# Last layer of a four-layer network: key times value formed in token rows, the scan banks filled by transposes that shift by one token

## The reference, cut to what matters

```python
def step(s, rkvw):
    r_t, k_t, v_t, w_t = rkvw
    a = k_t[:, :, :, None] * v_t[:, :, None, :]
    out = jnp.einsum('bhk,bhkd->bhd', r_t, u * a + s)
    return (a + w_t[:, :, :, None] * s, out)
```

## Time and profile before

| | us |
|---|---|
| runs shown: median (lowest to highest, 3 runs) | 1236.12 (1231.64 to 1236.43) |
| the profiled execution, its own time | 1234.46 |
| span of its profile | 1232.6 |
| PE busy in the span | 1107.8 (90%) |
| DVE busy | 837.0 (68%) |
| ACT busy | 541.0 (44%) |
| POOL busy | 426.9 (35%) |

### The profile page before, as it was taken

How to read it: one execution, slowest core, us unless ns; L and a number is a source line. 1 busy time by engine, 2 the same in 40 slices (tenths; PEclk the granted TensorE clock), 3 DMA queues, 4 the chain that set the end, 5 groups by cost and what they waited for, 6 DMA issues and landing times. The chain is left out here.

```text
span 1232.6 us, 21261 instructions
## 1 busy us (share of the span) xinstructions
PE 1107.8 (90%) x7840; PEld 703.0 (57%) x7840; DVE 837.0 (68%) x1609; ACT 541.0 (44%) x1000; POOL 426.9 (35%) x387
## 2 busy tenths in 40 slices
PE   7987788999999899999899899888998998989966
PEld 5875566568567567567567568564442433523414
DVE  4655766866866865866866866854467697695764
ACT  4643464473473473473473474441304314314221
POOL 2111444343343333343333333322335255164240
PEclk9979898999999999999999999999998999989988
DMA  7220100000001010102000000210010010000100
GB/s 243 64 91 18 40 1 23 18 18 19 20 17 56 17 60 17 34 17 87 19 17 21 17 17 18 71 62 18 1 35 19 1 36 18 18 19 1 34 1 17
DMA packets 37375, 40.73 MB, mean 33 GB/s; under 512 B 8064, under 2 KB 32832, under 8 KB 37072
## 3 DMA queue, kind: packets, MB, share of 16 engines
q1 hardware_dynamic: 37200, 40.01, 10.2%
q0 software_dynamic: 128, 0.10, 0.0%
HBM read 31.71 MB, written 8.39 MB: 33 GB/s over the span
## 5 line engine op out<-in xcount | busy, mean ns | idle before, releaser
L1349 DVE TENSOR_REDUCE b_neg_max<-head_area 128x16 f32<-128x1024 f32 x64 | 77.9, 1216 | 87.1 <-POOL head_area L784 86.7
L2054 POOL TENSOR_TENSOR c_rs<-c_st,head_area 128x512 f32<-128x512 f32 x64 | 82.2, 1286 | 129.9 <-DVE c_st L2462 129.9
L789 POOL TENSOR_TENSOR b_rstd<-b_var,minus_half 128x1 f32<-128x1 f32 x63 | 34.6, 549 | 256.6 <-DVE b_var L1378 256.6
L1032 PE MATMUL ps<-b_hT_mlp,wl 128*128 128x512 f32 x224 | 108.8, 608 | 8.4 <-ACT b_hT_mlp L1165 7.2
L1200 ACT ACTIVATE head_area<-head_area 128x1024 f32<-128x1024 f32 x64 | 68.0, 1062 | 102.2 <-DVE head_area L1354 101.6
L1046 PE MATMUL ps<-w,b_act_g 128*128 128x256 f32 x448 | 104.4, 387 | 2.7 <-ACT b_act_g L1218 2.7
L784 POOL TENSOR_TENSOR head_area<-head_area,b_self_add 128x1024 f32<-128x1024 f32 x32 | 75.7, 2366 | 81.7 <-DVE head_area L1342 81.7
L784 POOL TENSOR_TENSOR head_area<-head_area,b_cross_add 128x1024 f32<-128x1024 f32 x32 | 75.5, 2359 | 80.6 <-DVE head_area L1342 80.6
L1205 ACT ACTIVATE head_area<-ps 128x512 f32<-128x512 f32 x128 | 70.3, 605 | 63.9 <-PE ps L980 63.9
L1046 PEld LDWEIGHTS ps<-w,b_act_g 128*128 128x128 f32 x448 | 84.0, 193 | 18.1 <-issue 4.6
L865 PE MATMUL ps<-head_area,wl 128*128 128x512 f32 x176 | 86.2, 613 | 2.0 <-SPq L681 2.0
(11 more groups left out here) (252 smaller groups left out, 2319.8 us busy)
## 6 DMA issues: line engine op xcount, KB each, us to landing
b_x_in<-x_mid SPq DMA_DIRECT2D x9, 512.0 KB, 3.8
wl<-in_wl SPq DMA_DIRECT2D x4, 1024.0 KB, 6.8
head_area<-in_ctxT SPq DMA_DIRECT2D x8, 512.0 KB, 3.7
x_mid<-b_x_out SPq DMA_DIRECT2D x8, 512.0 KB, 2.9
area<-in_wc SPq DMA_DIRECT2D x1, 2336.0 KB, 8.3
a_x_in<-in_x SPq DMA_DIRECT2D x16, 128.0 KB, 3.1
a_y_in<-in_ctx SPq DMA_DIRECT2D x16, 128.0 KB, 3.5
w<-in_w SPq DMA_DIRECT2D x2, 1024.0 KB, 9.5
```

The source lines that it names most:

```text
L1032: mm = pe.matmul(ps[:, YB + j % 2, :], weight("w1", k, j * P, (j + 1) * P), hT_mlp[:, k, :], start=(k == 0), stop=(k == NC - 1))
L1349: dve.tensor_reduce(neg_max[:, k % 2, :], t, AX, ALU.max, negate=True).then_inc(max_ok, 1)
L2054: pool.tensor_tensor(rs[:, i % 4, :], st[:, i % 3, :], rF[:, i // RS, :], ALU.mult).then_inc(rs_ok, 1)
```

## The change

The product of k and v is formed with tokens on the rows, and the banks of the scan are filled by transposes of the product.

- ACT copies k and v without the extra column (`kF`, `vF`). PE transposes both to token rows (`to_tokens`, 4 transposes per chunk of channels, so 16 per head), and ACT copies these four outputs to `k_tok` and `v_tok` (`copy_tokens`). A head has 15 outputs, not 11. Both are placed in the turn and in the block between the phases.
- DVE forms the product of all 8 value channels for 128 tokens in one instruction of 128x1024 elements (both inputs repeated by their access patterns). The four instructions of the first chunk of channels stand in the turn before `own_weight`, those of the second chunk after the scans 0 to 3.
- `spread_v` with one selection product is replaced by `update` with four transposes. Their second operand is not the identity but `next_token`, which moves each token by one within its sequence. `key_value` on the PSUM bank is gone; the scan follows `start_state` directly.
- Two memsets (of `kS` and `vS`), the matrix `sel` (8 by 128 columns) and one semaphore of `phase_a` go. Some tiles of the middle layers move into shared areas; their waits stay as they were.

```diff
-HEAD = ("xx", "maa", "x5", "dec", "dexp", "decay", "kS", "vS", "rF", "gg", "ruk")
-OUTS = 11
+HEAD = ("xx", "maa", "x5", "dec", "dexp", "decay", "kF", "vF", "rF", "gg", "ruk", "k_tok", "v_tok", "kv1")
+OUTS = 15
+FIRST_OUT = {"k": 3, "k_tok": 5, "v": 7, "v_tok": 9, "r": 11, "g": 13}
...
 # phase_a: inv_ok joins xvn_ok
-                dve.reciprocal(inv, row_sum[:, p, :]).then_inc(inv_ok, 1)
-                dve.wait_ge(inv_ok, t + 1)
+                dve.reciprocal(inv, row_sum[:, p, :]).then_inc(xvn_ok, 1)
+                dve.wait_ge(xvn_ok, 2 * t + 1)
...
 # phase_c, bank_free (the block before phase_c alike)
-                    pe.wait_ge((k_ok, v_ok, r_ok)[(old - 3) // 2], NC * n + (old - 3) % 2 + 1)
+                    c = (old - 3) % 2 + 1
+                    if FIRST_OUT["k_tok"] <= old < FIRST_OUT["v"]:
+                        pe.wait_ge(tok_ok, 2 * NC * n + c)
+                    elif FIRST_OUT["v_tok"] <= old < FIRST_OUT["r"]:
+                        pe.wait_ge(tok_ok, 2 * NC * n + NC + c)
+                    else:
+                        pe.wait_ge({"k": k_ok, "v": v_ok, "r": r_ok}[...], NC * n + c)
...
-            def spread_v(n, i):
-                c = place(i)[0]
+            def to_tokens(n, src, done, m):
+                for c in range(NC):
+                    pe.wait_ge(done, NC * n + c + 1)
+                    bank_free(n, m + c)
+                    for p in range(NP):
+                        mm = pe.transpose(ps[:, PROJ + (m + c) % 2, p * P:(p + 1) * P], src[:, c, p * P:(p + 1) * P], w["ident"][:, :])
+                    mm.then_inc(proj_ps, 1)
+
+            def update(n, i):
+                c, d = i // RS, 2 * (i % 4) + i % RS // 4
                 if i >= 4:
                     pe.wait_ge(st_ok, NS * n + i - 3)
-                pe.matmul(seqs(ps[:, VB[i % 4], :]), w["sel"][:, i % RS, :], vS[:, c, :, 0:S], start=True, stop=True).then_inc(vb_ps, 1)
+                if i % RS == 0:
+                    pe.wait_ge(kv_ok, NC * NP * n + NP * (c + 1))
+                for p in range(NP):
+                    mm = pe.transpose(ps[:, VB[i % 4], p * P:(p + 1) * P], kv[c][:, p, d * P:(d + 1) * P], w["next_token"][:, :])
+                mm.then_inc(kv_ps, 1)
...
 # PE, turn of phase_c
                     mix_pair(n, 8)
+                    to_tokens(n, kF, k_ok, FIRST_OUT["k_tok"])
                     project(n, 2, "v")
                 if tail:
                     norm_T(1, last)
                 if head:
+                    to_tokens(n, vF, v_ok, FIRST_OUT["v_tok"])
                     project(n, 3, "r")
...
 # PE, block before phase_c
             hidden(6)
+            to_tokens(kF, k_ok, FIRST_OUT["k_tok"])
             project(2, "v")
             mix_pair(8)
+            to_tokens(vF, v_ok, FIRST_OUT["v_tok"])
             hidden(7)
...
 # ACT, turn of phase_c (the block before it alike, with gelu(0) and gelu(1) behind the copies)
-                    copy_projection(n, lambda c: kS[:, c, :, 1:S + 1], k_ok, 1)
-                    copy_projection(n, lambda c: vS[:, c, :, 1:S + 1], v_ok, 2)
+                    copy_projection(n, "k", kF, k_ok)
+                    copy_tokens(n, "k_tok", k_tok, tok_ok)
+                    copy_projection(n, "v", vF, v_ok)
+                    copy_tokens(n, "v_tok", v_tok, tok_ok)
                 if tail:
                     norm_out(1, last, "ln2_w", "ln2_b")
...
 # DVE
-            def key_value(n, i):
+            def key_value(n, c, tiles):
+                dve.wait_ge(tok_ok, 2 * NC * n + NC + c + 1)
+                for p in tiles:
+                    key = k_tok[:, c, p, :].rearrange("q (h k) -> q h k", h=HC).unsqueeze(1).broadcast_to([P, RS, HC, RS])
+                    value = v_tok[:, c, p, :].rearrange("q (d h) -> q d h", d=RS).unsqueeze(3).broadcast_to([P, RS, HC, RS])
+                    dve.tensor_tensor(kv[c][:, p, :].rearrange("q (d h k) -> q d h k", d=RS, h=HC), key, value, ALU.mult).then_inc(kv_ok, 1)
+
+            def scan(n, i):
+
+                dve.wait_ge(kv_ps, NS * n + i + 1)
                 dve.wait_ge(s0_ok, NS * n + i + 1)
-                kv = seqs(ps[:, VB[i % 4], :])
-                dve.tensor_tensor(kv, kv, kS[:, i // RS, :, 0:S], ALU.mult).then_inc(kv_ok, 1)
...
             def recurrence(n, nxt):
                 dve.wait_ge(decay_ok, 2 * NC * (n + 1))
-                key_value(n, 0)
                 for i in range(NS):
-                    if i + 1 < NS:
-                        key_value(n, i + 1)
                     scan(n, i)
+                    if KV2[0] <= i < KV2[0] + NP:
+                        key_value(n, 1, [i - KV2[0]])
...
                     ffn_mix(last)
                 if head:
+                    key_value(n, 0, range(NP))
                     own_weight(n)
                     gate(n)
...
-    lay["sel"] = np.stack([(i % HC == j // RS) & (i // HC == d) for d in [*range(0, RS, 2), *range(1, RS, 2)]], 1)
+    lay["next_token"] = (i // S == j // S) & ((i + 1) % S == j % S)
```

More of the change, by code:

```diff
@@ L1780, in _ @@
             decays()
-            copy_projection(lambda c: kS[:, c, :, 1:S + 1], k_ok, 1)
-            copy_projection(lambda c: vS[:, c, :, 1:S + 1], v_ok, 2)
+            copy_projection("k", kF, k_ok)
+            copy_tokens("k_tok", k_tok, tok_ok)
+            copy_projection("v", vF, v_ok)
+            copy_tokens("v_tok", v_tok, tok_ok)
             gelu(0)
             gelu(1)
-            copy_projection(lambda c: seqs(rF[:, c, :]), r_ok, 3)
+            copy_projection("r", rF, r_ok)
             gate_tanh()
@@ L1934, in phase_c @@
         minus_half, eps = sb("minus_half", NP), sb("eps", 1)
-        xx, maa, x5, dec, dexp, decay, kS, vS, rF, gg, ruk = (w[n] for n in HEAD)
+        xx, maa, x5, dec, dexp, decay, kF, vF, rF, gg, ruk, k_tok, v_tok, kv1 = (w[n] for n in HEAD)
+        kv = [kv1, sb("kv2", NP, RS * P)]
         ff_in = sb("ff_in", 2, NC, GT)
```

120 lines of the change are left out of this document (74 added, 46 removed).

## The result

The changed kernel took 1225.18 us (median of 4 runs, 1224.02 to 1226.71) against 1236.08 us before on the same chip: ratio 0.9927, 95% interval 0.9907 to 0.9948. A later comparison with 12 and 22 runs gave 0.9958 (0.9944 to 0.9972); one slow run of the kernel before (1612.93 us, clock 0.649) is left out of it. So the change gains 0.4 to 0.7%, about 5 to 9 us, where I had forecast 1237.0 with a lower end of 1227. The profiled execution took 1226.71 us, its span 1224.9.

A forecast was written before the change was run, and what follows sets the result against it. DVE was taken to bound the recurrences, PE the turns and block. Recurrences -11.5, turns +9.2, block +3.05 gave +0.7 us on 1234.46, so 1235.2; 1237 after the 1.7 us higher median. Range 1227 to 1248.

The forecast's parts named there:

- that term: First four steps of each recurrence: low clock makes first sums and bonus products late for DVE's bonus, 2.4 us lost.
- one of my own signs of a wrong forecast: Turns: the forecast would be wrong if they were longer by under 2 or over 4 us.
- Start: Start of each recurrence: first scan starts when DVE is free, 1.7 us saved four times, 6.8 us.
- First four steps: Scans 0 to 3: large DVE product plus POOL's product, 2.4 us a step; lower bound 2.26, upper 3.5.
- stall rival: First four steps: large products at the token shift's pace, 3.5 us a step, +17 us at worst, 1246 if half; chance 0.1.
- The body: Recurrence after the first steps: POOL at 1.25 us; low-rank input ends 26.7 us after first scan, saving 1.7 in groups 0 to 2.
- Turns: Three turns: PE's added transposes, bank wait and later `ffn_keys` make each 3.05 us longer, 9.2 us lost.
- block: Block before the last phase: transposes 1.85, bank wait 0.4, delayed gelus 0.8 us; 3.05 us lost.
- The slow one: Recurrences: PE at low clock needs 1.8 us a step; 14 us in all, median 1251, half way 1244; chance 0.2, mostly in part.
- the point I had named: Recurrence: the slow rival holds if the clock is not back by POOL's fourth product, at 10.7 us.
- The fast rival: Turns and block hide added work, growing 1.5 us, not 3.05, and the clock stays up at the start; 1228.5; chance 0.2.

The follow-up runs named there:

- filler: Changed kernel plus two unused PE products in PE's idle time ahead of the low-rank product, groups 0 to 2; 1226.74 us, ratio 0.9940 to the kernel before.
- the bonus products early: Changed kernel with PE's two bonus products moved ahead of the steps of a recurrence; 1226.05 us, ratio 0.9952 to the kernel before.
- both moves: Changed kernel with two of four large DVE products moved into the turn (groups 1 to 3) and PE's bonus products ahead of the steps; 1219.43 us, ratio 0.9894.
- few-transposes run: Changed kernel making only one of the four transposes of each update from step 8 on, all groups; 1227.65 us (one run).

## Why the prediction was wrong

The forecast was +0.7 us on the span, the profile shows -7.7. Of these 8.4 us, 4.3 are the clock, 1.8 a product of DVE that I left out of the sum, 1.1 lie before the last layer, and the remaining 1.2 are small errors of size (2.75 one way, 1.55 the other).

**The step that failed is the clock.** I wrote that it would fall in the first four steps and charged 0.6 us a group for it. It did fall there, for 7 us in groups 1 to 3 (1079.5 to 1086 in group 2) and for 3.5 in group 0, and in groups 1 to 3 the bonus waited 0.64, 0.55 and 0.64 us for PE: that term was right but for group 0, which had no wait. What I missed is that the low clock of before at the *end* of a recurrence, in a turn and in the tail was a cost that could go. I had rows of it, and used them only as a warning that the clock could get worse; in the sum it stood at nothing. Three terms of it went:

- Behind POOL's last product, 0.8 us: 0.5 in group 2 and 0.9 in group 3, less 0.6 more in group 0, where the low-rank product at the low clock ended after POOL's.
- The third turn, 1.7 us. Before, it had a low stretch at 1118.5 to 1122. It grew by 1.1 us where the second grew by 2.8, and by this it was one of my own signs of a wrong forecast.
- The tail, 1.8 us. Before, it was entered at the low clock (the last sums took 1.92 us, the mean 3.43; now 1.05 and 2.08).

0.8 + 1.7 + 1.8 = 4.3 us. The prices are shown by kernels whose code there is the same. Without the fall in group 0 (filler) the low-rank input to the mean took 4.73 us, not 5.45. The third turn, in the changed kernel and in the one with the bonus products early:
```profile
1106.84:1155.24 48.40, 44.57 (x151) 23.18 (x150) 30.66 (x59) 22.74 (x37) 14.51 (x14) 1.00 0.00 0
```
```profile
1108.07:1158.16 50.09, 46.26 (x150) 23.65 (x149) 30.81 (x59) 23.33 (x38) 14.48 (x14) 0.97 0.00 0
```
And the tail of the kernel with both moves, entered at the low clock as before the change, took as long as before the change:
```profile
1177.24:1219.28 42.04, 25.95 (x74) 15.64 (x72) 16.50 (x43) 12.68 (x20) 2.49 (x4) 0.80 0.04 12
```
The clock did not get better on the whole. The low stretches of the last layer add up to some 44 us before and 51 after; they lie where PE is not the path, as in the first four steps. Why they lie there is open. I thought of the second half of a recurrence as denser on PE: 2.15 us without work ahead of the sums of steps 12 and 13, not 2.72, and in group 3 1.40 ahead of each of the last, not 1.85 to 2.36. The few-transposes run shows that PE's transposes help to keep the clock up there. But groups 0 and 1 have the same 2.14 us and kept their low stretch (936 to 939.5, 1018 to 1021.5). So the denser work alone doesn't explain the gain, and luck may have a part in it: of the later kernels three had a third turn of over 52 us in their profiles.

**The product left out: 1.8 us.** I counted what DVE saves in groups 0 to 2 only up to the low-rank input (1.7 us a group). Behind it stood one more product of k and v, at a pitch of 0.60 us, ahead of the last two scans, POOL's last products and the mean. In group 3, where I counted to the end, it was in.

**Start: 5.3 us, not 6.8.** Group 0 gained 1.8 us. In groups 1 to 3 the scan starts 0.5 us after DVE is free: the first column of the scan stands on ACT behind `keep` (L2440), which waits for DVE's last output of the turn. I had counted ACT's column as done by then. A queued instruction that waits for the same engine was missed.

**First four steps.** The estimate of 2.4 us a step measured 2.25, the lower bound. I had DVE wait for POOL's product to end; the runs show the reverse: DVE issues first and POOL waits (1513 ns a product on the mean, 1286 before). The stall rival (the shift's pace, up to 17 us) needed the order that the shift has: there a second product with both inputs in SBUF follows on DVE, behind one of POOL, while in the first four steps a scan follows, which starts on time.

**The body** (1.1 us a group expected net of the late bonus; 2.05, 1.30 and 1.40 measured). I had POOL at 1.25 us as the pace. Seven scans ran at 1.13 without a wait, then one wait of 1.02 us came for ACT's column of scan 12, which stood behind ACT's two outputs of the next entry norm (1.45 us) and so behind PE's transposes for it, and the shift cost 2.53 us. With POOL's product halved the seven scans took the same 7.88 us, so POOL is not their bound.

**Turns: 2.84 and 2.82 us, not 3.05; block 3.13, not 3.05.** The mechanism was the one given: PE waits at `ffn_keys` 0.78 us and at the two banks 0.34 and 0.25, and 0.61 us ahead of the first MLP output in the block. I had expected 1.2 us at `ffn_keys`; it is less, by my reading since part of the delay was taken up by r's own wait ahead of it. Moving v's copies behind `norm_out` gave back 1.0 us, so this order was on the path. The four large products in the turn were hidden, as said, and two more were hidden as well.

**The rivals.** The slow one, PE at the low clock as the bound, shows for a short while in the few-transposes run: 2.7 us in group 0. In the change it did not happen; the clock was back at about the end of POOL's fourth product (1086 and 1085.3 in group 2), the point I had named. The fast rival (turns hide what is added) was wrong by its reason, though its time of 1228.5 was the nearest: the turns hid nothing, the clock did. The range ended at 1227 because no case in it let the clock gain.

Open: why the low stretches at the end of a recurrence and in the third turn went in some groups and not in others; and why the median of the changed kernel came out 1225.2 in one comparison and 1228.7, inside my range, in another, and spread over 9 us. The account above rests on the profiles and is the same for both. Two profiles of it differ only in the layers before the last. What decides the length of the low stretch near 70 us was not tried.

## What to carry to other kernels

When a change makes the work of PE denser or sparser in a stretch, price the low-clock stretches of the kernel before as terms of the sum, not only the ones that you expect to come: list them from the granted clock, say for each whether PE was on the path there, and ask which of them go. Follow a saving past the first place where another engine takes over, to the end of the stretch. When a move off one engine gives nothing, look for a second engine due at the same place: here neither of two moves gained alone, and together they took 7.4 us off the recurrences. An instruction that waits for an early engine must not be queued behind one that waits for a late one, as the bonus products behind POOL's sums and `norm_out` behind v's copies.

## What the hardware showed that I had not expected

With two SBUF inputs on both sides, a DVE product of 128x1024 kept its 1.20 us beside POOL, and a POOL product of 128x256 grew from 0.73 to 1.62 us. Which of the two pays is set by who is issued first. At the token shift DVE's two products of 128x512 took 2.53 us, where the two of the bonus (one input in PSUM) took 1.26; POOL's product was issued ahead of the second one, which took 1.75 us (group 2):
```profile
1098.52 1.71 POOL L2088 TENSOR_TENSOR c_rs<-c_st,head_area 128x512 f32<-128x512 f32 x1
```
```profile
1099.03 1.75 DVE L2485 TENSOR_TENSOR head_area<-head_area 128x512 f32<-128x512 f32 x1
```

Less work on PE made the last layer longer (388.4 us against 384.7, one profile each): with 24 transposes left out of each recurrence, group 0's took 2.7 us more through the clock, the others 0.6, 0.1 and 0.8.

Kernels that differ only in the last layer differed by up to 8 us ahead of it (834.5 to 842.6 us) in their profiles, with low stretches of 3 to 14 us near 70 us; the kernel before has one of 14 us.
